# Weight quantization gathered into the attention stage, activation quantization moved into the output projection

## What is computed

```python
xn   = layernorm(x)
q, k, v = xn @ Wq.T, xn @ Wk.T, xn @ Wv.T
kvt  = cumsum(k * v, axis=seq) * sqrt(D) / seq
attn = (q * kvt) @ Wo.T                                # "vhat" = q * kvt
bitlinear(a, w) = quant_act(a) @ quant_weight(w).T     # weights to -1, 0, 1 times mean|w|
h    = sigmoid(bitlinear(xn, Wgate)) * bitlinear(xn, Wup)
out  = x + attn + bitlinear(h, Wdown)
```

## Time and profile before

| | us |
|---|---|
| median of two timed runs | 11250.49 (11215.32 and 11285.67) |
| the profiled execution | 10772.67 |
| its span, slowest core | 10771.1 |
| spans of the eight cores | 10599.5 to 10771.1 |

### The profile page before, as it was taken

The page is one execution under the profiler, slowest core; times in us unless marked ns, Lnnn a source line. Parts: engine busy times, 40 slices in busy tenths (PEclk is TensorE's granted clock), DMA queues, the critical chain, the costliest instruction groups (busy, mean ns, idle before and its releaser), DMA issues.

```text
span 10771.1 us, 90685 instructions; the slowest of 8 cores (10599.5 to 10771.1 us)
## 1 busy us (share of the span) xinstructions
PE 7337.9 (68%) x31909; PEld 3381.4 (31%) x32530; DVE 3984.7 (37%) x4921; ACT 686.3 (6%) x1193; POOL 16.3 (0%) x20
## 2 busy tenths in 40 slices
PE   2999997287888788837762017999999544445555
PEld 1433443133333333313331013444444222222222
DVE  4344454523323323350003574222222444443333
ACT  3000000200000000000000001000000000000000
POOL 0000000000000000000000000000000000000000
PEclk9988898598998999868886558999999766677777
DMA  1344554123223223351124632121211444444454
GB/s 67 129 156 133 165 168 137 48 73 108 79 83 108 96 75 99 104 163 61 55 77 142 186 106 85 70 85 70 85 70 59 146 139 140 141 162 151 166 166 158
DMA packets 484980, 1214.02 MB, mean 113 GB/s; under 512 B 39986, under 2 KB 203954, under 8 KB 462002
## 3 DMA queue, kind: packets, MB, share of 16 engines
q1 hardware_dynamic: 339378, 990.02, 28.5%
q10 hardware_dynamic: 142848, 201.39, 5.1%
q0 software_dynamic: 2304, 16.78, 0.8%
HBM read 989.93 MB, written 218.10 MB: 112 GB/s over the span
## 4 chain that ended last, share of the span: by engine, by line
PE 57%; DVE 18%; DMA 17%; issue 4%; ACT 2%; ACTq 1%; DVEq 1%; SPq 0%; POOL 0%; POOLq 0%
PE pb L419 9%; PE pb L422 9%; PE pb L426 9%; PE pb L828 8%; PE pb L823 8%; PE pb L997 5%; DMA S<-wd_s 5%; DMA wd_s<-A 4%; DMA wg_s<-A 3%; PE pb L965 2%; DVE A L291 2%; DMA wu_s<-A 2%; PE pb L673 2%; PE pb L676 2%; PE pb L681 2%
## 5 line engine op out<-in xcount | busy, mean ns | idle before, releaser
L419 PE MATMUL pb<-S,A 128*128 128x512 bf16 x5017 | 1973.5, 393 | 520.1 <-DVE A L403 359.0
L422 PE MATMUL pb<-S,A 128*128 128x512 bf16 x5018 | 1972.5, 393 | 40.1 <-DVE A L403 22.5
L426 PE MATMUL pb<-S,A 128*128 128x512 bf16 x5017 | 1969.0, 392 | 6.3 <-issue 0.6
L828 PE MATMUL pb<-S 128*128 128x512 bf16 x4096 | 1554.0, 379 | 9.8 <-ACT S L772 1.3
L823 PE MATMUL pb<-S 128*128 128x512 bf16 x3932 | 1491.7, 379 | 0.0
L997 PE MATMUL pb<-S 128*128 128x512 bf16 x4008 | 934.1, 391 | 160.3 <-DMA S<-wd_s 138.1
L965 PE MATMUL pb<-id32s,A 128*128 128x128 f32 x1024 | 248.1, 423 | 1068.6 <-DVE A L954 1068.6
L419 PEld LDWEIGHTS pb<-S,A 128*128 128x128 bf16 x5120 | 514.8, 101 | 1212.8 <-issue 699.2
L291 DVE TENSOR_TENSOR A<-A 128x1024 bf16<-128x1024 bf16 x384 | 265.9, 692 | 1293.9 <-DMA wu_s<-A 865.6
L426 PEld LDWEIGHTS pb<-S,A 128*128 128x128 bf16 x5120 | 515.3, 101 | 651.4 <-issue 134.5
L422 PEld LDWEIGHTS pb<-S,A 128*128 128x128 bf16 x5120 | 514.2, 100 | 641.8 <-issue 127.0
(11 more groups left out here) (102 smaller groups left out, 4752.1 us busy)
## 6 DMA issues: line engine op xcount, KB each, us to landing
S<-wd_s SPq DMA_DIRECT2D x128, 2048.0 KB, 8.9
A<-wg SPq DMA_DIRECT2D x256, 512.0 KB, 4.8
A<-wu SPq DMA_DIRECT2D x256, 512.0 KB, 4.9
A<-wd SPq DMA_DIRECT2D x256, 512.0 KB, 5.3
h_s<-A ACTq DMA_DIRECT2D x256, 256.0 KB, 2.0
A<-h_s SPq DMA_DIRECT2D x128, 512.0 KB, 3.7
A<-xm SPq DMA_DIRECT2D x48, 1024.0 KB, 5.0
A<-wk SPq DMA_DIRECT2D x32, 1024.0 KB, 7.5
```

Of the source, the lines that this page charges most:

```text
L419: e.matmul(pb[c][:, :], whi[p][:, dt * 128:(dt + 1) * 128], S1[:, mv:mv + 512], start=s, stop=False))
L422: e.matmul(pb[c][:, :], whi[p][:, dt * 128:(dt + 1) * 128], S2[:, mv:mv + 512], start=False, stop=False))
L426: e.matmul(pb[c][:, :], wlo[p][:, dt * 128:(dt + 1) * 128], S1[:, mv:mv + 512], start=False, stop=s))
L828: e.matmul(pb[pr * 2 + 1][:, :], S1[:, stat:stat + 128], wu_sl[sl][:, dt * 512:(dt + 1) * 512], start=s, stop=p))
```

## The change

- `quant_step` behind a block of stage 3 takes 24 units instead of 13, so all 384 units are done in stage 3; stage 4 has none.
- Wo is laid out by blocks of 512 output columns (`wo_d[fc]`, 128 x 8192). Stage 4 loops first over the two pairs of such blocks and inside over the 8 groups of tokens. Before each pair its part of Wo is loaded in 8 pieces of 1 MB through one buffer and split, both parts into `S2`. The pieces wait for the matmuls and transposes issued before them.
- `vhat_s` is loaded for each pair and group: 16 times 32 loads instead of 8 times 32.
- Behind the matmuls of each of the 16 iterations stands `prep_step(2)`: one tile of 128 tokens of the former stage 5, into `S1`, which is free now. It has one buffer for x and one for the result (`c5`) where there were two each.
- `stage4` has four buffers instead of eight. The barrier now lies behind prep, so the first `load_gu` come after it.

```diff
-            quant_step(len(q_units) // (2 * NE) + 1)
+            quant_step((len(q_units) + NE - 1) // NE)
...
         phase_barrier()
-        for et in range(NE):
...
-            quant_step(1)
+        quant_step(len(q_units))
...
+        def prep_step(n):
...
+                if s == 0:
+                    wait("sync", svv, pstate["x_free"])
+                    pstate["x_load"] = stX.dma(
+                        x5[:, 0:D], xm_d[tt * 128:(tt + 1) * 128, 0:D])
+                wait_t("vector", pstate["x_load"])
...
+                op("vector", lambda e: e.tensor_copy(r5, AI[:, 0:QW]))
+                wait("vector", ssc, pstate["af_free"])
+                op("vector", lambda e: e.scalar_tensor_tensor(
+                    out=c5, in0=t5, scalar=-0.5, in1=r5,
+                    op0=ALU.add, op1=ALU.is_gt))
...
+        for pi, fcl in enumerate(fc_pairs):
+            spl_done = 0
+            for c2 in range(len(fcl)):
+                fc = fcl[c2]
+                for hhalf in range(NE * 512 // 2048):
+                    wait("sync", svv, spl_done)
+                    wait("sync", smm, wo_sweep_done)
+                    lt = stWO.dma(wo_in[:, 0:2048],
+                                  wo_d[fc, :, hhalf * 2048:(hhalf + 1) * 2048])
+                    wait_t("vector", lt)
+                    wait("vector", smm, wo_sweep_done)
...
+            pair_split_done = spl_done
+            for ttg in range(NTTG):
+                wait("sync", smm, pstate.get("vs_free", 0))
+                for et in range(NE):
+                    stVR.dma(vs_hi[:, et * 256:(et + 1) * 256],
+                             vhat_d[0, et, :, ttg * 256:(ttg + 1) * 256])
+                    stVR.dma(vs_lo[:, et * 256:(et + 1) * 256],
+                             vhat_d[1, et, :, ttg * 256:(ttg + 1) * 256])
+                wait_all("tensor", stVR)
+                wait("tensor", svv, pair_split_done)
...
-                quant_step(2)
-            stat_free = smm.c
+                pstate["vs_free"] = smm.c
+                prep_step(n_prep_per_iter)
+            wo_sweep_done = smm.c
         ph4_mm = smm.c
-        quant_step(len(q_units))
-        q8_all = stQ8W.all_toks()
-        gu_done = qu["gu_done"]
-
-        phase_barrier()
...
+        prep_step(len(prep_units))
         prep_done_sc = ssc.c
         prep_done_vv = svv.c
 
+        phase_barrier()
```

More of the change, by code:

```diff
@@ L616, in build_program @@
                 next_split = stream_weight_split(wq_d, e + 1, 0)
-            quant_step(len(q_units) // (2 * NE) + 1)
+            quant_step((len(q_units) + NE - 1) // NE)
         ph3_mm = smm.c
         phase_barrier()
-        wo_in = [A32[:, 0:2048], A32[:, 2048:4096]]
-        stage4 = A32[:, 4096:8192]
-        wo_free = [0, 0]
-        for et in range(NE):
[L626 to L637, removed]
-            quant_step(1)
-        wo_split_done = svv.c
+        quant_step(len(q_units))
+        wo_in = A32[:, 0:2048]
+        stage4 = A32[:, 2048:4096]
+        x5sl = [A32[:, 4096:6144]]
+        t5 = A32[:, 6144:6144 + QW]
+        c5 = A32[:, 7168:7168 + QW]
+        d5 = A32[:, 8192:8192 + QW]
+        r5 = A32[:, 9216:9216 + QW]
+        NSL = D // QW
         vs_hi = A16[:, 0:NE * 256]
@@ L644, in build_program @@
         NFCW = D // 512
-        stat_free = 0
-        bank_free4 = [(0, "ssc")] * 8
[L647 to L659, removed]
+        prep_units = [(tt, s) for tt in range(NT) for s in range(NSL)]
@@ new lines, in build_program @@
+        fc_pairs = [tuple(range(p, min(p + 2, NFCW)))
+                    for p in range(0, NFCW, 2)]
+        bank_free4 = [(0, "ssc")] * 8
+        stage_free = [None] * 4
+        wo_sweep_done = 0
+        n_prep_per_iter = max(1, (len(prep_units) + len(fc_pairs) * NTTG - 1)
+                              // (len(fc_pairs) * NTTG))
+        for pi, fcl in enumerate(fc_pairs):
[9 more added lines that the diff above has]
+                    wait("vector", smm, wo_sweep_done)
+                    base = c2 * 2 * NE * 512 + hhalf * 2048
+                    op("vector", lambda e, base=base:
+                       e.tensor_copy(S2[:, base:base + 2048], wo_in[:, 0:2048]))
+                    spl_done = op("vector", lambda e, base=base:
+                                  e.scalar_tensor_tensor(
+                                      out=S2[:, NE * 512 + base:
+                                             NE * 512 + base + 2048],
+                                      in0=wo_in[:, 0:2048], scalar=0.0,
+                                      in1=S2[:, base:base + 2048],
+                                      op0=ALU.add, op1=ALU.subtract), svv)
+            pair_split_done = spl_done
[8 more added lines that the diff above has]
+                wait("tensor", svv, pair_split_done)
@@ L689, in build_program @@
                 for tl in range(2):
-                    for c2, fc in enumerate(fcl):
+                    for c2 in range(len(fcl)):
+                        fc = fcl[c2]
                         bkk = tl * 2 + c2
-                        si = (bkk + hf * 4) % 8
+                        si = bkk
                         wait("scalar", smm, mt)
@@ L715, in build_program @@
[L715 to L770, removed]
-                    ev = op("scalar", lambda e, tb=tb, dst=dst:
-                            e.copy(out=dst, in_=pb[4 + tb][:, 0:512]), ssc)
-                    tb_free[tb] = ev
-                    af_free[asl] = ev
@@ L789, in build_program @@
         wgu_free = [0, 0]
-        for tok in q8_all:
-            wait_t("sync", tok)
-        wait_t("sync", gu_done)
         gu_load_t = {}
```

73 lines of the change are left out of this document (61 added, 12 removed).

## The result

| | before | after |
|---|---|---|
| timed runs, median | 11215.32 (25 runs) | 11250.68 (26 runs) |
| profiled execution, its span | 10771.1 | 10765.8 |
| ratio of after to before | | **1.0067, 95% interval 1.0038 to 1.0096** |

The changed kernel is 0.67% slower, about 72 us of 10700 (41 to 103). That is under the 2% named in the prediction, and yet clear of no change.

A forecast was written before the change was run, and what follows sets the result against it. The quantization chain was taken as what K waits for in stage 3. Added units +709 us, and 590 us saved from there to stage 6, gave +119 on the median 11250.5: 11370 us, range 10860 to 11600.

The forecast's parts named there:

- What bounds stage 3: Stage 3: K waits for the quantization chain, about 11 us to spare on PE, so added units are wholly exposed.
- added units are hidden under PE: Faster rival, stage 3: the added units' 709 us would shrink; fully hidden, 10660 us; chance 0.05.
- Price of a unit: Stage 3: each added quantization unit costs 3.75 us for Wu and 4.13 us for Wd.
- part 1: Stage 3: 176 more units, 48 of Wu (180 us) and 128 of Wd (529 us), cost +709 us.
- 14 gaps: Stage 4, between iterations within the pairs: PE waits 25 us each for reloaded vhat, 350 us in all.
- change of pair: Stage 4, between the two pairs of Wo blocks: PE idle 102 us for transposes, Wo splits and vhat loads.
- tail: End of stage 4: prep's second unit, the barrier and the gate and up weights take 36 us after the last matmul.
- bound of 22 us for gaps: Stage 4, lower side of the range: vhat gaps of 22 us without quantization traffic would take off 42 us more.
- likeliest case: Whole kernel: +119 us, bounds about 0 to +200, 11265 to 11450 from the median, within 2%; chance 0.68.
- slow rivals: Stages 3 and 4: prep not hidden, 11500 us, or quantization slower in its new place, 11505 us; chance 0.12 each.
- Prep is not hidden: Slower rival, stage 4: prep's x and two units follow the matmuls and end the gaps, adding 128 us, 11500; chance 0.12.
- Quantization slower in its new place: Slower rival, stage 3: loads pace Wd's units; at 4.8 us 176 units cost 845 us, total 11505; chance 0.12.

The follow-up runs named there:

- part 2 alone: Changed kernel with 13 units behind each block again, the other 176 worked off in a row before the splits of Wo: 10761 us, ratio to before 1.0108.
- the other placement: Changed kernel with its 24 units per block placed 8 behind the block and 4 behind each copy of K, split of Wv ahead: 9838 us, ratio 0.922.
- the experiment: Changed kernel with each 256 KB store of a Wd unit issued as two of 128 KB; executed once for its profile, not timed further.
- part 1 alone: Kernel before with 24 units behind each block of stage 3, none left for stage 4, loop order and prep as before: 10800 us, +118 to before.

## Why the prediction was right or wrong

**What bounds stage 3: right.** K waits for the chain of units. The two ways to reach it, split and copy, both appear in the waits, part 2 alone shows that a unit costs there what it costs in an idle stretch, and the other placement, by taking away 902 us, that the order was the cause. That the rival *added units are hidden under PE* got 0.05 was as it should be.

**Price of a unit: the term that was mis-sized in part 1.** +691 instead of +709. Counted over whole blocks in core 0, an added unit of Wg or Wu cost 3.70 us (the first ten blocks grew by 406.6 us for 110 units), where I took 3.75, and one of Wd 4.02 (the last six blocks grew by 284.6 us, with 128 of Wd and 16 others in the place of 78 of Wu), where I took 4.13. The step that failed is that I read Wd's price from the working-off of core 0 alone, the dearest core of eight, and put it down to the larger store. That reason fell with the experiment. The page of the Trainium skill cited in the prediction ("DMA: Bandwidth & Descriptors", "Anatomy of one DMA") describes DMAs that GpSimd issues, while these stores are issued by ACT. By it a store would gain nothing from being split, and the trace agrees; by it Wd's units would also go at Wu's pace, and in core 0 they don't (4.02 against 3.70).

**Stage 4: nearly right, most terms a little too large.** The 14 gaps took 344 us against 350, the matmuls 43.2 us an iteration against 43.7, which is 7 us in all, PE's start 85.8 us against 89. The rest held: Wo pieces 8.7 against 8.85, change of pair 102 against 102, prep's second unit 16 us behind the matmuls against 16, tail 37 against 36. Together 1276 predicted, 1259.9 measured. The bound of 22 us for gaps "with no quantization traffic beside them" had no ground: in part 1 alone, with no unit in stage 4, the seven gaps still took 24.8 us in the mean ((353.3 - 202.0 + 22.6)/7), against 25.2 before.

**The difference.** +119 against about +72. Of the 47 us between, 18 are the units and 16 the stretch after stage 3; the remaining 13 are within the interval of the measurement. The bound of 0 to +200 held it.

**Where it failed: the base and the verdict.** The sum was put on a wrong base. I took 10772.7 for the kernel before, and this holds the 81 us that cores 0 and 1 lost in stage 1; the other six cores, with spans from 10599.5 to 10678.9, had not lost them. The comparable executions before have a median of 10715. With +119 that gives 10834, not 10892, and the changed kernel came in at 10759 to 10805, median 10786: below the range of 10860 to 11600 that was to hold a run like the profiled one. That the median of all 26 runs, 11250.7, lies in the range is luck, since the base of two runs (11250.5) became 11215 with 25, and the runs after scatter from 10759 to 11481. The second step is the verdict. 2% was called about what a measurement can tell from no change, and with "no change" at 0.70 the likeliest statement was that nothing would be seen. The runs tell 0.67% from none. The sign was right, and the likeliest case's own range (11265 to 11450, against a base of 11250) lay wholly on the slower side; it should have been read as "slower, by less than 2%".

**The slow rivals** had 0.24 and neither came. *Prep is not hidden*: 6.7 us to spare at the least, 9 computed. *Quantization slower in its new place*: counted as above, Wd's units cost 3.7 to 4.2 us in stage 3 over the eight cores and 3.75 to 4.13 in the working-off, far from 4.8. Both had a computed margin against them and were still given prices near the border; the margins were sound.

## What to carry to other kernels

Ask of work put beside matmuls not whether its engine is idle, but what stands behind it in the engine's stream and in that of whoever stores its results; here the same 384 units made 902 us of difference by their place alone. A wait has layers (vhat 24.6, prep 16.3, bank copies 5.6 us): compute the next one before taking the first away, and expect a second link (here a shared semaphore) under a buffer. And compare a stage that the change doesn't touch, and the other cores, before you compare two spans or take one as a base: here one stage of two cores hid the whole difference.

## What the runs showed of the hardware

A store of 256 KB split into two of 128 KB on two semaphores did not get faster: the wait per unit was 1.8 to 2.1 us over the cores instead of 1.5 to 1.8. A unit that moves 512 KB in and 256 KB out did not get under 3.37 us in the mean with two load buffers, with 0.2 us of waiting for stores left, while DVE's own part is 2.5; its loads (Wg, Wu) then took 4.8 us to land instead of 3.7, its stores 4.3 instead of 2.3. The same row of units costs up to 10% more on one pair of cores than on another in one execution (4.13 and 3.75 us before), and both cores of a pair show the same. Work on DVE and the DMA engines beside the matmuls (DMA busy 0.51, DVE 1141 of 2133 us in the kernel with units between K and V) did not lengthen the matmuls: 141.6 us a block for 576 matmuls at 0.216 us, which is 124.2, and 15.7 of waiting.
